# Self attention's first loads in order of use, with a semaphore for each group, in a two-layer decoder on one core

## The chip, the cores and the metric

The kernel runs on one core of one Trainium2 chip. The metric is the device time of one execution in microseconds; lower is better. All loads and stores of the part that matters here are issued by SyncE (SP) and are carried by the core's 16 DMA engines, which work through them while TensorE (PE), VectorE (DVE), ScalarE (ACT) and GpSimd (POOL) compute.

## The reference

The model is a decoder of two layers on x of 16 batches, 100 tokens and 256 features. Each sublayer adds its result to x and normalises. The parts run one after the other: self attention with four branches, cross attention, an expert adapter, a second attention in buckets, a latent attention and a routed feed-forward layer. The change touches only the first part (and the place where the last part's buffer is set to zero):

```python
q = (X @ Wq + bq).reshape(B, T, H_TOT, DH).transpose(0, 2, 1, 3)   # 64 heads of 16
v = (X @ Wv + bv).reshape(B, T, H_TOT, DH).transpose(0, 2, 1, 3)
k_base = (X @ Wk + bk).reshape(B, T, N_HEAD, DH).transpose(0, 2, 1, 3)
k = jnp.tile(k_base, (1, N_BR, 1, 1))
q = _rope(q); k = _rope(k)
scores = einsum('bhtd,bhsd->bhts', q, k) * ATTN_SCALE
w = jax.nn.softplus(scores / sqrt(clip(sum(k * k), 1e-06)))
w = jnp.where(causal, w, 0.0); w = w * jax.nn.sigmoid(SCALE * w)
sinks = jnp.tanh(sink_scalars) + 1e-06
alpha = 1.0 / (jnp.sum(w, axis=-1, keepdims=True) + sinks + 1e-06)
context = einsum('bhts,bhsd->bhtd', w * alpha, v) + sinks * alpha * v_nulls
y = context @ Wo + bo        # then the mean over the four branches
```

So k needs Wk, bk and the tables of the rotation, q needs Wq and bq, v needs Wv and bv, the scores need two masks, and the end of a batch needs Wo, bo, the sinks and v_nulls.

## The kernel before

Everything is float32 and is held in SBUF: `X` is [128, 16, 256], one batch per middle index. `build` (L2739 and on) first opens a block of its own ("io"). There DVE sets the tile `zero` to 0 (L2754), and SP issues the identity matrix `ident` (L2758), the whole of x (L2759, 1,600 KB), and then twenty stores of `zero` (L2762, 128 KB each) that clear `rows_in`, the DRAM buffer of the routed layer, which is used only at the end of the kernel. SP then waits for x (`s_in`), and the block ends with a barrier of all engines.

`self_attention` follows. SP issues 16 loads (L281), all on one semaphore `s_w`, then the operands of cross attention and of the router (L86). At their heads PE, DVE, ACT and POOL each wait for the full count of `s_w` (`16 * NW`): PE ahead of `x_turned(0)`, DVE after ten memsets and ahead of the constants, ACT ahead of the Tanh of the sinks (L676), POOL ahead of `staged(0)` (L683), which copies a batch of x for PE to transpose. DVE's constants are `odd` (L607), `sink` and `csk` (L608, L609) and `csvn` (L611, L613).

Then `four_in_flight` runs the same body on each engine, o = -3, -2, -1, 0 written out, ten in a hardware loop of two, five written out. In one body four batches are in work at different steps: F projects k and q of batch o + 3 and applies the rotation (POOL), S makes scores and masks of batch o + 2 and projects v, V multiplies the gated weights with v, O sums and normalises. The body o = -3 holds F alone, o = -2 holds F and S. On PE the body o = -3 is `k_projected` (L298), `q_projected` (L306), `k_turned` (L325), `q_turned` (L334), and the transposition of the next batch (L291); the body o = -2 begins with `scores` (L350). On DVE a body's order is masks, bias of k (L461), bias of q (L474), the sum of squares of k (L466, L468), masks (L500), v with its bias (L492), `kT_read` (L482), `xT_read` (L455), softplus (L507). On ACT: the copy of q (`qT_read`, L622), sigmoid (L629), logarithm (L633), gate (L637). The order on every engine is that of the program text; nothing is scheduled by a tool.

Of the kernel before, what the change touches and what calls it, by code (L numbers as in the profile page):

```python
# [14 lines left out]
P = 128  # L15
NB, T, D = 16, 100, 256
KD = D // P
NH = 16
# [179 lines left out]
def self_attention(nc, X, ident, d, later):  # L198
# [13 lines left out]
    with st:  # L212
# [35 lines left out]
        s_w, s_c = sem("weights_loaded"), sem("consts_ready")  # L248
# [17 lines left out]
        NW = 16  # L266

        with nc.Block() as block:
            @block.sync
            def _(sp):  # L270
                for dst, src in ((wk[:], rows(d["L0_attn_Wk"])), (bk[:], bcast(d["L0_attn_bk"], T)),
                                 (wq[:], rows(d["L0_attn_Wq"])), (bq[:], bcast(d["L0_attn_bq"], T)),
                                 (cos[:], d["c_cos"]), (sin[:], d["c_sin"]), (odd[:], d["c_odd"]),
                                 (wv[:], rows(d["t_L0_attn_Wv"])),
                                 (bv[0:HK, :], bcast(d["t_L0_attn_bv"][0, :], HK)),
                                 (bv[HK:P, :], bcast(d["t_L0_attn_bv"][1, :], HK)),
                                 (mask_a[:], d["c_mask_a"]), (mask_b[:], d["c_mask_b"]),
                                 (wo[:], rows(d["t_L0_attn_Wo"])), (bo[:], bcast(d["L0_attn_bo"], T)),
                                 (sink[:], bcast(d["t_L0_attn_sinks"], T)),
                                 (csvn[:], bcast(d["t_L0_attn_v_nulls"], T))):  # L280
                    sp.dma_start(dst, src).then_inc(s_w, 16)  # L281
                for w in later:
                    w.load(sp)

            @block.tensor
            def _(pe):
# [111 lines left out]
                def body(o, par):  # L398
                    N, F, S, V, O = parts(o)
                    f, s, v = o + 3, o + 2, o + 1  # L400
                    other = (par + 1) % 2
                    if S:
                        scores(s, par, 0)
# [40 lines left out]
                pe.wait_ge(s_w, 16 * NW)  # L444
# [4 lines left out]
            def _(dv):  # L449
# [99 lines left out]

                def body(o, par):  # L550
                    N, F, S, V, O = parts(o)
                    f, s, v = o + 3, o + 2, o + 1
                    other = (par + 1) % 2
                    if S:
                        masked(s, 0)
# [10 lines left out]
                    if F:  # L566
                        q_biased(f, 1)
                        k_summed(f)
                    if S:
                        masked(s, 2)  # L570
                        masked(s, 3)
# [24 lines left out]

                cs.start(0)
                for b in range(2):
                    nc.vector.memset(xT[b][:], 0.0)
                    nc.vector.memset(kTm[b][:], 0.0)  # L600
                    cs.after(nc.vector.memset(va[b][:], 0.0))
                    nc.vector.memset(va[b][:, :, :, DH:DH + 1], 1.0)
                nc.vector.memset(half[:], -0.5)
                cs.after(nc.vector.memset(tiny[:], 1e-37))
                dv.wait_ge(s_w, 16 * NW)
                dv.wait_ge(s_c, 1)
                cs.after(nc.vector.tensor_scalar(odd[:], odd[:], DH ** -0.5, None, ALU.mult))  # L607
                cs.after(nc.vector.tensor_scalar(sink[:], sink[:], 1e-6, None, ALU.add))  # L608
                cs.after(nc.vector.tensor_scalar(csk[:], sink[:], 1e-6, CS, ALU.add, ALU.mult))  # L609
                v3 = csvn[:, :].rearrange("p (h c) -> p h c", c=DH)  # L610
                cs.after(nc.vector.tensor_tensor(v3, v3, sink[:, :].unsqueeze(2).broadcast_to([T, NBR * NH, DH]),  # L611
                                                 ALU.mult))
                cs.after(nc.vector.tensor_scalar(csvn[:], csvn[:], CS, None, ALU.mult))  # L613
# [4 lines left out]
            def _(ac):  # L618
# [56 lines left out]
                ac.wait_ge(s_w, 16 * NW)  # L675
                nc.scalar.activation(sink[:], sink[:], ACT.Tanh).then_inc(s_c, 1)  # L676
# [3 lines left out]
            def _(po):  # L680
# [65 lines left out]
                def body(o, par):  # L746
                    N, F, S, V, O = parts(o)
                    f, s, v = o + 3, o + 2, o + 1
                    if F:
                        k_roped(f)  # L750
# [14 lines left out]
                po.wait_ge(s_w, 16 * NW)  # L765
                staged(0)
                four_in_flight(po, body)
# [1973 lines left out]
def build(nc, d, out):  # L2741
# [4 lines left out]
    with st:  # L2746
        X = st.sb("X", [P, NB, D])
        ident, zero = st.sb("ident", [P, P]), st.sb("zero", [P, D])
        s_in = st.sem("x_loaded")
        s_z, s_zero = st.sem("zero_ready"), st.sem("rows_zeroed")  # L2750
        with nc.Block() as block:
            @block.vector
            def _(dv):
                nc.vector.memset(zero[:], 0.0).then_inc(s_z, 1)  # L2754

# [82 lines left out]
```

## Time and profile before

| | us |
|---|---|
| median of 3 runs | 2407.62 (2407.28 to 2408.91) |
| the profiled execution | 2405.48 |
| its span, first to last instruction | 2403.8 |
| PE busy | 2046.5 (85% of the span) |
| the first projection starts at | 43.83 |

The profile has one execution. Its times count from the first instruction; 1.68 us of the profiled execution lie outside the span. Engines are named as above; SPq is SyncE's queue, whose instructions here only issue DMAs.

### The profile page before, as it was taken

The page shows a single profiled execution, that of the slowest core. Times are in us where ns is not written, and L with a number is a line of the kernel's source. Part 1 is how long each engine was busy: PE and PEld are TensorE (multiplying, and loading weights), DVE is VectorE, ACT ScalarE, POOL GpSimd, SP SyncE. Part 2 cuts the span into 40 slices and gives each one's busy share as a digit, 9 for nine tenths or more (in the row PEclk, how much of TensorE's full clock was granted, in tenths as well). Part 3 has the DMA queues.
Part 4 walks back from the last instruction along what each step waited for, and adds up shares of the span by engine and source line. Part 5 has one row for each costly group of instructions (what it writes and reads, how often), then busy time and mean ns, then how long its engine had stood idle before and what let it go on. Part 6 is the DMA issues. An engine that isn't in the chain of part 4 may idle for free. (4 is left out here: it accounts for less than half of the span.)

```text
span 2403.8 us, 48411 instructions
## 1 busy us (share of the span) xinstructions
PE 2046.5 (85%) x17362; PEld 1267.9 (53%) x17363; DVE 1345.4 (56%) x3265; ACT 1118.3 (47%) x2404; POOL 482.6 (20%) x583
## 2 busy tenths in 40 slices
PE   1788878869999997878879999999999999955991
PEld 0444445545666664645545555555555556543671
DVE  2577778744555555479954555555555555541223
ACT  0676677734555553346644444544444454420110
POOL 2566655510101000155520000000000000002002
PEclk9899999868999997889989999999999999967996
DMA  6000000003121000000000000000000000053102
GB/s 163 1 2 1 0 0 0 2 15 87 45 83 38 12 12 1 1 1 0 0 7 11 10 7 6 6 6 6 6 6 6 12 6 1 1 186 142 33 30 60
DMA packets 50463, 60.85 MB, mean 25 GB/s; under 512 B 9849, under 2 KB 44974, under 8 KB 49918
## 3 DMA queue, kind: packets, MB, share of 16 engines
q1 hardware_dynamic: 47366, 53.74, 7.2%
q0 software_dynamic: 3008, 5.91, 0.8%
q8 instruction: 57, 0.93, 0.2%
q14 instruction: 32, 0.26, 0.0%
HBM read 51.11 MB, written 8.52 MB: 25 GB/s over the span
## 5 line engine op out<-in xcount | busy, mean ns | idle before, releaser
L2011 PE MATMUL la_side<-la_wkv,la_inT 128*128 128x512 f32 (+1 forms) x512 | 243.8, 599 | 0.0
L2289 ACT COPY la_pT<-la_pPT 128x400 f32<-128x400 f32 x246 | 122.0, 496 | 257.4 <-PE la_pPT L2042 256.9
L1999 PE MATMUL la_side<-la_inT,la_wkv 128*128 128x461 f32 x512 | 225.6, 564 | 0.8 <-ACT la_inT L2264 0.8
L2179 DVE CUSTOM_DVE_ANT_0 la_pr<-la_pS,la_mb 100x461 f32<-100x461 f32 x256 | 148.1, 636 | 130.3 <-PE la_pS L2029 130.3
L2280 ACT ACTIVATE la_pr<-la_pr,la_nm 100x461 f32<-100x461 f32 x256 | 172.5, 681 | 0.0
L2353 POOL TENSOR_TENSOR la_xb<-io_X,la_bo 100x256 f32<-100x256 f32 x16 | 11.7, 730 | 784.2 <-DVE io_X L2168 784.2
L1020 DVE TENSOR_REDUCE ca_nm<-ca_pS 100x2 f32<-100x722 f32 x128 | 116.2, 908 | 85.9 <-PE ca_pS L907 84.1
L2042 PEld LDWEIGHTS la_pPT<-io_ident,la_pr 100*128 100x128 f32 x984 | 110.1, 141 | 102.5 <-issue 97.4
L2141 DVE COPY la_v<-la_side 128x512 f32<-128x512 f32 (+1 forms) x128 | 88.3, 690 | 130.9 <-PE la_side L2011 129.6
L1092 ACT ACTIVATE ca_pr<-ca_pS,ca_nm 100x361 f32<-100x361 f32 x256 | 130.0, 561 | 64.5 <-DVE ca_nm L1020 62.7
L2042 PE MATMUL la_pPT<-io_ident,la_pr 100*128 100x100 f32 x984 | 125.4, 249 | 1.4 <-issue 1.4
L1999 PEld LDWEIGHTS la_side<-la_inT,la_wkv 128*128 128x128 f32 x512 | 89.1, 193 | 67.2 <-issue 66.5
L2011 PEld LDWEIGHTS la_side<-la_wkv,la_inT 128*128 128x128 f32 (+1 forms) x512 | 82.7, 179 | 77.6 <-issue 77.6
L2029 PE MATMUL la_pS<-la_kT,la_qT 64*100 64x461 f32 x512 | 115.9, 571 | 0.0
L2268 ACT COPY la_kT<-la_side 128x461 f32<-128x461 f32 x128 | 68.8, 538 | 96.0 <-PE la_side L1999 96.0
L907 PE MATMUL ca_pS<-ca_kT,ca_qTm 32*100 32x361 f32 x512 | 110.2, 506 | 0.3
L2052 PEld LDWEIGHTS la_pav<-la_pT,la_v 128*64 128x64 f32 x2048 | 90.2, 137 | 37.9 <-issue 33.5
L2189 DVE TENSOR_SCALAR la_pr<-la_pr,la_zs 100x461 f32<-100x461 f32 x256 | 106.4, 458 | 4.5
L2052 PE MATMUL la_pav<-la_pT,la_v 128*64 128x100 f32 x2048 | 103.5, 253 | 3.1 <-ACT la_pT L2289 2.7
L1760 ACT ACTIVATE ba_pr<-ba_A,ba_mx 100x100 f32<-100x100 f32 x256 | 75.8, 367 | 53.1 <-DVE ba_mx L1702 53.1
L372 PEld LDWEIGHTS sa_pb<-sa_L,sa_va 64*32 64x32 f32 x4096 | 69.9, 110 | 53.8 <-issue 53.8
L916 PE MATMUL ca_pPT<-io_ident,ca_pr 100*128 100x100 f32 x768 | 88.5, 251 | 4.3 <-DVE ca_pT L1027 2.5
(360 smaller groups left out, 4225.7 us busy)
## 6 DMA issues: line engine op xcount, KB each, us to landing
rf_w<-in_L_ffn_W SPq DMA_DIRECT2D x16, 1024.0 KB, 13.2
ca_cn<-in_ctx SPq DMA_DIRECT2D x16, 256.0 KB
far_cn<-in_ctx SPq DMA_DIRECT2D x16, 256.0 KB, 2.7
rows_in<-io_zero SPq DMA_DIRECT2D x20, 128.0 KB, 4.7
rb_xr<-rows_in POOLq DMA_DIRECT2D x20, 128.0 KB, 2.3
rows_out<-rb_yr SPq DMA_DIRECT2D x20, 128.0 KB, 1.7
ea_wcT<-in_t_L_ffn_conv_W SPq DMA_DIRECT2D x1, 2048.0 KB
la_wkv<-in_L_xattn_Wkv SPq DMA_DIRECT2D x1, 2048.0 KB
```

The source lines that it names most:

```text
L907: last = nc.tensor.matmul(pS[0:T, 2 * (m % 2) + e, 0:SC], qTm[b][rows_, h // HG, h % 2, :], kT[b][rows_, h // HG, :], start=True, stop=True)
L1020: nc.vector.reduce_max(nm[m % 2][:], pS[0:T, 2 * (m % 2):2 * (m % 2) + 2, 0:SC], AX, negate=True)\
L1092: ins = nc.scalar.activation(pr[m % NP][:, e, 0:SC], pS[0:T, 2 * (m % 2) + e, 0:SC], ACT.Exp, bias=nm[m % 2][:, e:e + 1])
L1999: last = nc.tensor.matmul(pf[:, 0:SK], wkv[:, k, e * P:(e + 1) * P], inT[:, k, :], start=k == 0, stop=k == KD - 1)
L2011: last = nc.tensor.matmul(pf[0:keys[c], :], inT[:, k, c * P:c * P + keys[c]], wkv[:, k, o:o + 512], start=k == 0, stop=k == KD - 1)
L2029: last = nc.tensor.matmul(o[e], qT[b][half[e], m, :], kT[b][half[e], m, :], start=True, stop=True)
L2042: last = nc.tensor.transpose(dst[:, c * T:(c + 1) * T], pr[m % 4][:, e, c * P:(c + 1) * P], ident[0:T, 0:T])
L2052: last = nc.tensor.matmul(pav[DX * e:DX * (e + 1), m % 4, :], v[b][:, c, (2 * m + e) * DX:(2 * m + e + 1) * DX], pT[m % 2][:, e, c * T:(c ...
L2179: ins = nc.vector.tensor_tensor_reduce(out=pr[m % 4][:, e, 0:SK], in0=pS[0:T, 2 * (m % 2) + e, 0:SK], in1=mb[b][:, :], scale=-1.0, scalar= ...
L2189: ins = nc.vector.tensor_scalar(pr[m % 4][:, e, 0:SK], pr[m % 4][:, e, 0:SK], zs[m % 2][:, 2 + e:3 + e], None, ALU.mult)
L2280: ins = nc.scalar.activation(pr[m % 4][:, e, 0:SK], pr[m % 4][:, e, 0:SK], ACT.Exp, scale=-1.0, bias=nm[m % 2][:, e:e + 1], accum_out=zs[m ...
L2289: nc.scalar.copy(pT[m % 2][:, e, :], src[:, 0:NC * T]).then_inc(s_PT, 1)
```

## The change

Self attention takes over the io block's work, so that block and its barrier are gone. SP now issues, on seven semaphores: `ident` and batches 0 and 1 of x (`s_x0`); Wk, bk, cos, sin, odd (`s_lk`); Wq, bq (`s_lq`); Wv, bv, the masks (`s_lv`); the other 14 batches of x (`s_xl`); Wo, bo, sinks, v_nulls (`s_lo`); the operands of later stages as before; and the twenty stores of `zero` last. PE and POOL start on `s_x0`; the body o = -3 (`begin`) waits for k's and q's groups, the body o = -2 (`second`) for the rest. The memsets of `va` move into DVE's body o = -3, the constants from the sinks and v_nulls into its body o = -2, the Tanh to the head of ACT's body o = -2.

```diff
         with nc.Block() as block:
             @block.sync
             def _(sp):
+                xt = d["x"].rearrange("b t d -> t b d")
+                sp.dma_start(ident[:], d["c_ident"]).then_inc(s_x0, 16)
+                sp.dma_start(X[0:T, 0:2, :], xt[:, 0:2, :]).then_inc(s_x0, 16)
                 for dst, src in ((wk[:], rows(d["L0_attn_Wk"])), (bk[:], bcast(d["L0_attn_bk"], T)),
...
+                sp.dma_start(X[0:T, 2:NB, :], xt[:, 2:NB, :]).then_inc(s_xl, 16)
...
                 for w in later:
                     w.load(sp)
+                sp.wait_ge(s_z, 1)
+                for k in range(NBK):
+                    sp.dma_start(rows_in[k * P:(k + 1) * P, :], zero[:]).then_inc(s_zero, 16)
...
             def _(pe):
...
+                    if begin:
+                        pe.wait_ge(s_lk, 16 * 5)
+                        pe.wait_ge(s_lq, 16 * 2)
+                    if second:
+                        pe.wait_ge(s_lv, 16 * 5)
+                        pe.wait_ge(s_lo, 16 * 4)
...
-                pe.wait_ge(s_w, 16 * NW)
+                pe.wait_ge(s_x0, 32)
                 x_turned(0)
                 four_in_flight(pe, body)
...
             def _(dv):
...
+                def values_prepared():
+                    for b in range(2):
+                        cs.after(nc.vector.memset(va[b][:], 0.0))
+                        cs.after(nc.vector.memset(va[b][:, :, :, DH:DH + 1], 1.0))
+
+                def sinks_prepared():
+                    dv.wait_ge(s_lo, 16 * 4)
+                    dv.wait_ge(s_c, 1)
...
                     if F:
                         q_biased(f, 1)
                         k_summed(f)
+                    if begin:
+                        values_prepared()
+                    if second:
+                        sinks_prepared()
                     if S:
                         masked(s, 2)
...
             def _(ac):
...
+                    if isinstance(o, int) and o == FIRST + 1:
+                        ac.wait_ge(s_lo, 16 * 4)
+                        nc.scalar.activation(sink[:], sink[:], ACT.Tanh).then_inc(s_c, 1)
                     if V:
...
             def _(po):
...
+                    if second:
+                        po.wait_ge(s_xl, 16)
+                        po.wait_ge(s_lo, 16 * 4)
...
-                po.wait_ge(s_w, 16 * NW)
+                po.wait_ge(s_x0, 32)
                 staged(0)
+                po.wait_ge(s_lk, 16 * 5)
                 four_in_flight(po, body)
...
-        s_in = st.sem("x_loaded")
-        s_z, s_zero = st.sem("zero_ready"), st.sem("rows_zeroed")
-        with nc.Block() as block:
...
-                sp.dma_start(X[0:T, :, :], d["x"].rearrange("b t d -> t b d")).then_inc(s_in, 16)
-                sp.wait_ge(s_z, 1)
-                for k in range(NBK):
-                    sp.dma_start(rows_in[k * P:(k + 1) * P, :], zero[:]).then_inc(s_zero, 16)
-                sp.wait_ge(s_in, 32)
```

On SP, the queue from its start. Names are destination and source; `x19` is nineteen alike; before:

```order
L2758 DMA io_ident<-in_c_ident 128x128
L2759 DMA io_X<-in_x 100x16x256
L2762 DMA rows_in<-io_zero 128x256 [waits io_zero_ready]
L2762 DMA rows_in<-io_zero 128x256 x19
L2751 UNCONDITIONAL_BRANCH [waits io_x_loaded]
L269 UNCONDITIONAL_BRANCH [waits barrier_Pool_Activation_PE_DVE_SP_release]
L281 DMA sa_wk<-in_L_attn_Wk 128x2x256
L281 DMA sa_bk<-in_L_attn_bk 100x256
L281 DMA sa_wq<-in_L_attn_Wq 128x2x1024
L281 DMA sa_bq<-in_L_attn_bq 100x1024
```

and in the changed kernel:

```order
L274 DMA io_ident<-in_c_ident 128x128
L275 DMA io_X<-in_x 100x2x256
L278 DMA sa_wk<-in_L_attn_Wk 128x2x256
L278 DMA sa_bk<-in_L_attn_bk 100x256
L278 DMA sa_cos<-in_c_cos 100x8
L278 DMA sa_sin<-in_c_sin 100x8
L278 DMA sa_odd<-in_c_odd 128x2
L280 DMA sa_wq<-in_L_attn_Wq 128x2x1024
L280 DMA sa_bq<-in_L_attn_bq 100x1024
```

Wk was behind all of x, twenty stores, a wait and a barrier; it is now behind the identity and two batches of x.

On DVE, from the last setup to the first mask of the body o = -2, before:

```order
L607 TENSOR_SCALAR sa_odd<-sa_odd 128x2 [waits sa_consts_ready,sa_weights_loaded,sa_setup_chain]
L608 TENSOR_SCALAR sa_sink<-sa_sink 100x64 [waits sa_setup_chain]
L609 TENSOR_SCALAR sa_csk<-sa_sink 100x64 [waits sa_setup_chain]
L611 TENSOR_TENSOR sa_csvn<-sa_csvn,sa_sink 100x1024 [waits sa_setup_chain]
L613 TENSOR_SCALAR sa_csvn<-sa_csvn 100x1024 [waits sa_setup_chain]
L455 COPY sa_xT<-sa_pk 128x2x100 [waits sa_xT_in_psum,sa_setup_chain]
L461 TENSOR_TENSOR sa_kn<-sa_pk,sa_bk 100x256 [waits sa_k_in_psum]
L474 TENSOR_TENSOR sa_qn<-sa_pq,sa_bq 100x512 [waits sa_q_in_psum] x2
L466 TENSOR_REDUCE sa_kss<-sa_ksq 100x16 [waits sa_k_squares]
L468 TENSOR_SCALAR sa_kss<-sa_kss 100x16 [waits sa_k_sum_chain]
L482 TENSOR_TENSOR sa_kTm<-sa_pk,sa_odd 128x2x128 [waits sa_kT_in_psum]
```

and in the changed kernel, the same stretch:

```order
L648 TENSOR_SCALAR sa_odd<-sa_odd 128x2 [waits sa_k_operands_loaded,sa_setup_chain]
L474 COPY sa_xT<-sa_pk 128x2x100 [waits sa_xT_in_psum,sa_setup_chain]
L480 TENSOR_TENSOR sa_kn<-sa_pk,sa_bk 100x256 [waits sa_k_in_psum,sa_q_operands_loaded]
L493 TENSOR_TENSOR sa_qn<-sa_pq,sa_bq 100x512 [waits sa_q_in_psum] x2
L485 TENSOR_REDUCE sa_kss<-sa_ksq 100x16 [waits sa_k_squares]
L487 TENSOR_SCALAR sa_kss<-sa_kss 100x16 [waits sa_k_sum_chain]
L571 MEMSET sa_va 128x2048
L572 MEMSET sa_va 128x64 [waits sa_setup_chain]
L571 MEMSET sa_va 128x2048 [waits sa_setup_chain]
L572 MEMSET sa_va 128x64 [waits sa_setup_chain]
L501 TENSOR_TENSOR sa_kTm<-sa_pk,sa_odd 128x2x128 [waits sa_kT_in_psum,sa_setup_chain]
```

The four constants are gone from ahead of the first copy of x, and four memsets stand between the sum of squares of k and `kT_read`.

On DVE in the body o = -2, in the changed kernel; before, the mask L500 (here L519) followed the sum of squares directly:

```order
L485 TENSOR_REDUCE sa_kss<-sa_ksq 100x16 [waits sa_k_factors,sa_k_squares]
L487 TENSOR_SCALAR sa_kss<-sa_kss 100x16 [waits sa_k_sum_chain]
L577 TENSOR_SCALAR sa_sink<-sa_sink 100x64 [waits sa_consts_ready,sa_out_operands_loaded]
L578 TENSOR_SCALAR sa_csk<-sa_sink 100x64 [waits sa_setup_chain]
L580 TENSOR_TENSOR sa_csvn<-sa_csvn,sa_sink 100x1024 [waits sa_setup_chain]
L582 TENSOR_SCALAR sa_csvn<-sa_csvn 100x1024 [waits sa_setup_chain]
L519 TENSOR_TENSOR sa_sm<-sa_pS,sa_mask_a 128x800 [waits sa_scores_in_psum,sa_setup_chain]
```

The four constants now stand ahead of the masks of the third and fourth chunk.

## Rows read from the trace of the kernel before

**Rows 1.** Timeline, 0 to 31 us: start us, duration us, engine, line, operation.
```profile
1.02 0.27 DVE L2754 MEMSET io_zero<- 128x256 f32 x1 [1.02 <-PEq L2826]
1.35 0.39 SPq L2759 DMA_DIRECT2D io_X<-in_x  x1
1.80 14.73 SPq L2762 DMA_DIRECT2D rows_in<-io_zero  x20
16.98 0.40 SPq L281 DMA_DIRECT2D sa_wk<-in_L_attn_Wk  x1
...
20.27 0.27 DVE L599 MEMSET sa_xT<- 128x256 f32 x1
...
27.13 2.99 SPq L281 DMA_DIRECT2D sa_csvn<-in_t_L_attn_v_nulls  x1
```

**Rows 2.** Waits, 0 to 200 us: waiter, releaser, us, times, longest.
```profile
POOL sa_xs L683 <- DMA sa_csvn<-in_t_L_attn_v_nulls: 39.8, 1, 39.8
```

**Rows 3.** Timeline, 18 to 66 us: start, duration, engine, line, [idle before, releaser].
```profile
18.30 1.76 DVE L601 MEMSET sa_va<- 128x2048 f32 x1 [0.38 <-issue]
...
40.38 0.40 POOL L683 COPY sa_xs<-io_X 100x256 f32<-100x256 f32 x1 [39.79 <-DMA sa_csvn<-in_t_L_attn_v_nulls]
...
41.42 1.23 DVE L611 TENSOR_TENSOR sa_csvn<-sa_csvn,sa_sink 100x1024 f32<-100x1024 f32 x1
...
42.68 0.69 DVE L613 TENSOR_SCALAR sa_csvn<-sa_csvn 100x1024 f32<-100x1024 f32 x1
...
43.83 2.03 PE L298 MATMUL sa_pk<-sa_wk,sa_xT 128*100 128x256 f32 x4 [2.34 <-DVE sa_xT L455]
...
52.09 1.04 DVE L468 TENSOR_SCALAR sa_kss<-sa_kss 100x16 f32<-100x16 f32 x1
...
58.64 0.64 DVE L482 TENSOR_TENSOR sa_kTm<-sa_pk,sa_odd 128x256 f32<-128x256 f32 x2 [5.51 <-PE sa_pk L325]
...
65.79 1.34 PE L350 MATMUL sa_pS<-sa_qT,sa_kTm 32*128 32x144 f32 x16 [0.67 <-ACT sa_qT L622]
```

**Rows 4.** Windows: us, POOL busy (x), PEclk, DMA share, GB/s.
```profile
2.00:7.00 5.00, 0.00 (x0) 1.00 0.65 160
12.00:17.00 5.00, 0.00 (x0) 1.00 0.98 330
17.00:40.00 23.00, 0.00 (x0) 1.00 0.96 251
```

**Rows 5.** DMA issues: count, KB each, median us to landing.
```profile
rows_in<-io_zero SPq DMA_DIRECT2D x20, 128.0 KB, 4.7
io_X<-in_x SPq DMA_DIRECT2D x1, 1600.0 KB
```

**Rows 6.** Timeline of the body o = -2, 67 to 88 us.
```profile
67.98 0.68 ACT L629 ACTIVATE sa_L<-sa_sm 128x576 f32<-128x576 f32 x1 [1.03 <-DVE sa_sm L500]
...
74.93 1.30 POOL L729 TENSOR_TENSOR sa_qb<-sa_qn,sa_sin 100x512 f32<-100x512 f32 x1
...
82.39 1.26 ACT L633 ACTIVATE sa_L<-sa_L,sa_tiny 128x1152 f32<-128x1152 f32 x1
...
85.06 1.59 PE L334 MATMUL sa_pq<-io_ident,sa_qr 100*128 100x100 f32 x8 [4.80 <-POOL sa_qr L740]
...
86.69 0.83 ACT L622 COPY sa_qT<-sa_pq 128x800 f32<-128x800 f32 x1 [3.04 <-PE sa_pq L334]
```

**Rows 7.** Timeline, the same DVE line in two places, 100 to 107 us.
```profile
100.28 0.42 DVE L525 TENSOR_TENSOR sa_num<-sa_num,sa_alpha 100x256 f32<-100x256 f32 x1
...
105.41 1.30 POOL L736 TENSOR_TENSOR sa_qa<-sa_qn,sa_sin 100x512 f32<-100x512 f32 x1
...
105.70 1.29 DVE L525 TENSOR_TENSOR sa_num<-sa_num,sa_alpha 100x256 f32<-100x256 f32 x1
```

**Rows 8.** Windows, fill and loop: PE, PEld, DVE, ACT, POOL busy (x), PEclk, DMA share, GB/s.
```profile
40.40:66.00 25.60, 10.47 (x30) 5.45 (x34) 7.03 (x14) 1.37 (x3) 14.97 (x17) 0.80 0.05 11
...
154.00:198.00 44.00, 35.85 (x633) 22.18 (x632) 33.98 (x70) 30.65 (x33) 27.29 (x27) 1.00 0.01 2
```

More of the change, by code:

```diff
@@ L195, in four_in_flight, with self_attention @@
         body(o, o % 2)
-def self_attention(nc, X, ident, d, later):
+def self_attention(nc, X, ident, d, later, zero, rows_in, s_zero):
     CS = float(np.pi / np.sqrt(3.0))
@@ L246, in self_attention @@
         pb = ps("pb", [P, 512])
-        s_w, s_c = sem("weights_loaded"), sem("consts_ready")
+        s_x0, s_xl = sem("first_x_loaded"), sem("x_loaded")
+        s_lk, s_lq, s_lv, s_lo = (sem(f"{n}_operands_loaded") for n in ("k", "q", "v", "out"))
+        s_c, s_z = sem("consts_ready"), sem("zero_ready")
         s_xs, s_xTp, s_xT = sem("xs_staged"), sem("xT_in_psum"), sem("xT_ready")
@@ L401, in body @@
                     other = (par + 1) % 2
+                    begin, second = isinstance(o, int) and o == FIRST, isinstance(o, int) and o == FIRST + 1
+                    if begin:
[4 more added lines that the diff above has]
+                        pe.wait_ge(s_lo, 16 * 4)
                     if S:
@@ L548, in normed @@
                         .then_inc(s_x, 1)
+                def values_prepared():
[5 more added lines that the diff above has]
+                    dv.wait_ge(s_c, 1)
+                    cs.after(nc.vector.tensor_scalar(sink[:], sink[:], 1e-6, None, ALU.add))
+                    cs.after(nc.vector.tensor_scalar(csk[:], sink[:], 1e-6, CS, ALU.add, ALU.mult))
+                    v3 = csvn[:, :].rearrange("p (h c) -> p h c", c=DH)
+                    cs.after(nc.vector.tensor_tensor(v3, v3, sink[:, :].unsqueeze(2).broadcast_to([T, NBR * NH, DH]),
+                                                     ALU.mult))
+                    cs.after(nc.vector.tensor_scalar(csvn[:], csvn[:], CS, None, ALU.mult))
                 def body(o, par):
@@ L553, in body @@
                     other = (par + 1) % 2
+                    begin, second = isinstance(o, int) and o == FIRST, isinstance(o, int) and o == FIRST + 1
+                    if begin:
+                        dv.wait_ge(s_lq, 16 * 2)
+                    if second:
+                        dv.wait_ge(s_lv, 16 * 5)
                     if S:
@@ L595, in body @@
                         softplus(s, par, 2)
+                nc.vector.memset(zero[:], 0.0).then_inc(s_z, 1)
                 cs.start(0)
@@ L599, in _ @@
                     nc.vector.memset(xT[b][:], 0.0)
-                    nc.vector.memset(kTm[b][:], 0.0)
-                    cs.after(nc.vector.memset(va[b][:], 0.0))
-                    nc.vector.memset(va[b][:, :, :, DH:DH + 1], 1.0)
+                    cs.after(nc.vector.memset(kTm[b][:], 0.0))
                 nc.vector.memset(half[:], -0.5)
                 cs.after(nc.vector.memset(tiny[:], 1e-37))
-                dv.wait_ge(s_w, 16 * NW)
-                dv.wait_ge(s_c, 1)
+                dv.wait_ge(s_lk, 16 * 5)
                 cs.after(nc.vector.tensor_scalar(odd[:], odd[:], DH ** -0.5, None, ALU.mult))
[L608 to L613, printed above, removed]
                 xT_read(0, 0)
@@ L748, in body @@
                     f, s, v = o + 3, o + 2, o + 1
+                    second = isinstance(o, int) and o == FIRST + 1
+                    if second:
+                        po.wait_ge(s_xl, 16)
+                        po.wait_ge(s_lo, 16 * 4)
                     if F:
```

29 lines of the change are left out of this document (13 added, 16 removed).

## The prediction

> **What bounds the kernel at its start.** I read SyncE's queue first, then the waits, then the timeline of the first body. SyncE issues x at 1.35 us, then spends 14.73 us on the twenty stores of zeros (1.80 to 16.53), and the weights' first load leaves only at 16.98 [rows 1]. The waits say who suffers: POOL's first copy of x, and all behind it, waits 39.8 us for one load, v_nulls, the last of the sixteen that share one semaphore [rows 2]. In the timeline the last load has landed just ahead of 40.38, and PE's first projection starts at 43.83, 3.4 us later: between them stand the copy of x, its transposition, and DVE's constants, of which the last ends at 43.37 [rows 3]. So the kernel computes nothing of use in its first 43.83 us. What follows is a chain of stages with a barrier after each, none of which waits for something with a time of its own. Whatever the first projection gains, the end gains, less what the fill gives back.
>
> **Part 1: when k's and q's operands are there.** From the shapes (a tile's partitions times elements times 4 bytes; two of the sizes are in [rows 5]) the bytes ahead of `s_lq` are: identity 64 KB, two batches of x 200, Wk 256, bk 100, three small tables 7, Wq 1,024, bq 400: 2,051 KB or 2.10 MB. All six groups up to v_nulls are 5,580 KB, 5.71 MB. Before, 2,560 KB (2.62 MB) of zeros went with them, and everything had landed at 40.2.
>
> First what the removal of the zeros is worth. In the stretch 12 to 17 us, which is zeros almost alone, 330 GB/s moved [rows 4]: 2.62 MB are 7.9 us. So the last group should land at 40.2 - 7.9 = 32.3 us; SyncE's first load leaves at about 1 us as before and moves its first bytes at about 2.0. That is 5.71 MB in 30.3 us, 188 GB/s. The first 2.10 MB at that rate take 11.2 us and land at 13.2. At the 251 GB/s of the stretch 17 to 40 us [rows 4] they take 8.4 us and land at 10.4. The stretch 2 to 7 us, x almost alone, moved only 160 GB/s with a DMA share of 0.65 [rows 4], so I stay near the slow end: 12.5, with 10.4 and 13.2 as near bounds. A far bound: the three stretches of [rows 4] moved 0.80, 1.65 and 5.77 MB, and the one between them (7 to 12 us), at 160 to 330 GB/s, 0.8 to 1.65: by 40 us 9.0 to 9.9 MB had moved, against 8.34 MB issued up to v_nulls. So some 1.1 MB of later loads were ahead of it, and a group doesn't land strictly first; 1.1 MB more at 188 GB/s make 19.
>
> The DMA share of 0.65 with x alone [rows 4] is what 10 busy engines of 16 give. The Trainium skill (DMA: Bandwidth & Descriptors, "Why a DMA increments its semaphore by 16 and not by 1") says that a transfer with 100 partitions is split over 10 engines and one with 128 over 16, and the trace agrees. By that rule the ten engines carry 155 KB each up to `s_lq` and 447 KB each up to `s_lo`; 155/447 of 30.3 us would be 10.5 us, a landing at 12.5. By bytes alone it is 13.2; the page would leave the sum where it is.
>
> What else stood ahead of the projection is covered: the identity and two batches of x (264 KB) land at some 4 us, so POOL's copy, PE's transposition and DVE's memsets (all but `va`'s) are done long before 12.5, and the small k group lands before the large q group. The first projection starts at 12.6 instead of 43.83: **31.2 us gained**.
>
> **Part 2: the second body's wait.** PE waits for `s_lv` and `s_lo` at the head of the body o = -2, ahead of `scores`. Behind it in its queue are the scores, the k and q projections and everything that feeds DVE and POOL. ACT waits for `s_lo` after its first copy of q. These stood at 65.79 [rows 3], 21.96 us after the first projection, so they come up at 12.6 + 22.0 = 34.6. The last group lands at 32.3 by part 1: 2.3 us early, cost nothing. This cover is thin. The gain at that point is 65.8 less the later of (the landing of `s_lo`) and (the landing of `s_lq` + 22.1). If q's group comes at 10.4 the second wait binds, and the gain is 33.5 and not more; if `s_lo` comes at 36 it is 29.8. POOL's wait for `s_xl` and `s_lo` has more room: its next work is the first multiplication after the bias of k, well after the scores.
>
> **Part 3: DVE's memsets of `va` in the body o = -3.** Two of 1.76 us [rows 3] and two small ones (64 elements each, under the 0.27 us of a memset of 256 [rows 1]), with their chain waits some 4.2 us. They start when the sum of squares ends, at 53.13, and DVE was idle from there until 58.64, 5.51 us [rows 3]. 5.5 against 4.2 to 4.9: cost 0. If each stood behind a POOL operation of 1.3 us once, they would end up to 1 us late: bound 1.0.
>
> **Part 4: the constants in the body o = -2.** Before, the two long ones ran from 41.42 to 43.37 [rows 3], with the two small ones ahead of them 2.4 us in all, after POOL's copy. Now they run from about 75.0 (times of before) beside POOL's 1.30 us multiplication at 74.93 [rows 6]. The pair L525/L736 shows what that does: the same DVE operation takes 0.42 us alone and 1.29 beside POOL's, ending when POOL's ends [rows 7]; L468, a sum's clip over 16 elements, takes as much as 1.04 beside POOL in the first body [rows 3]. So the masks behind the constants move by 2.4 to 3.7 us. Who waits: the scores of the third group on PE, then sigmoid and logarithm on ACT. ACT's logarithm ended at 83.65 and ACT then idled 3.04 us until the copy of q at 86.69 [rows 6]. The shift is at most 3.5 there (0.2 is taken up by DVE's own idle time): 0 to 0.5 us too late. The other way round, DVE's two long operations (1.23 and 0.69 [rows 3]) can hold up POOL, and PE does wait for POOL's chain (4.80 us ahead of L334) [rows 6]: up to 1.9 us. I take 0.5 for both together, near the low end, since POOL's next operation after 76.2 reads only 16 elements a partition.
>
> The Trainium skill (SBUF — State Buffer, the part on the shared port pair) says that a DVE operation with two SBUF inputs, or a `tensor_scalar` in the fast mode, and a GpSimd operation that reads SBUF exclude each other, while a memset doesn't contend. The 1.29 of [rows 7] agrees; that a memset is free of it no row shows. By the page part 3 costs nothing and part 4 is as above.
>
> **Part 5: what moves without a price.** The Tanh (0.26 us) stands before the first sigmoid, for which ACT waited 1.03 us [rows 6]; no table load is added. The zeros leave at some 35 to 50 us, behind the operands of later stages; nobody needs them before the last stage. The DMA queue is then full while bodies -3 to -1 run; before, it was nearly idle there (share 0.05 [rows 8]). DVE's memset of 256 elements took 0.27 us both at 1.02, before any byte had moved, and at 20.27 in the full stretch [rows 1, 4], so I put nothing on it. Below zero nothing is to be had: no operation left out was on the path apart from those of part 1.
>
> **The sum.** 31.2 - 0.5 = 30.7 us. The profiled execution, 2405.48 with a span of 2403.8, becomes 2374.8 with a span of 2373.1. The median of the runs is 2.14 us above the profiled execution, 2407.62; it becomes **2376.9 us**.
>
> **The rivals.**
> 1. *The second wait takes the place of the first.* The last group lands later than 34.6, since the first 25 us now hold only loads and no fast zeros. For it: the margin is 2.3 us out of 32. Against it: the same loads with the zeros between them took 40.2. Landing at 36 to 38 gives a gain of 29.8 to 27.8, less 0.5: 2378.3 to 2380.3. It decides from 34.6 on.
> 2. *The fill gives back more.* Parts 3 and 4 at their upper bounds (1.0 + 0.5 + 1.9 = 3.4), or PE's clock comes up later in the first body (there it was granted 0.80 on average [rows 8], between its two levels of 1.2 and 2.4 GHz; eight q matmuls at most 1.7 us slower). Gain 31.2 - 3.4 = 27.8: 2379.8.
> 3. *The groups don't land apart.* If the queue works on all issued loads at once, q's group lands almost with the last, at 32.3, and only the zeros and the constants are saved: 43.83 - 32.4 = 11.4 us gained: 2396.2. For it: the 1.1 MB of part 1 that overtook. Against: that is an eighth of the traffic then, not all of it.
> 4. *Slower.* The loop of self attention loses its clock. It runs at 1.00 with PE busy 35.85 of 44 us [rows 8]. PE rests longer ahead of its first work in one piece no more, but the fill now begins with a transposition at 4 us and a pause until 12.6; if the grant in the loop fell to the lower level, the 35.85 us would become 71.7, 27.7 us more than the stretch of 44. It would turn the gain into a loss after some 49 us of such running: 2,407 and above, 2420 for 70 us. Against it: before, the clock came up after a far longer pause.
>
> **How the numbers follow.** The forecast 0.70, second wait 0.12, fill 0.10, groups together 0.05, slower 0.03. The forecast's own bounds: gain 33.5 (q at 10.4) less 0 is 2374.1; q at 13.2 with 1 us of fill is 2378.1; another 1 us on both sides for clock and run. The range of 8 in 10 takes in rivals 1 and 2: 2373 to 2381. A measurement of this kernel can tell about 0.2% (4.8 us) from no change; only rival 4 reaches that bound from the other side: faster 0.96, same 0.01, slower 0.03.
>
> **What will show it.** Right: the first projection at 12.6 (10.4 to 13.3) with PE released by a load of the q group; SyncE's zeros last; the scores L350's counterpart at 34.6 released by ACT's copy of q and not by a DMA; ACT's idle before the second copy of q down from 3.0 to near 0; the memsets done before `kT_read`; everything from 110 us on as before, 30.7 earlier. Wrong: a DMA as releaser at the scores (rival 1), POOL operations of over 1.3 us beside DVE's constants or a late `kT_read` (rival 2), the projection after 20 us (rival 3), a PEclk below 1.00 in the loop (rival 4).

## The result, and the profile after

The changed kernel takes **2384.57 us** (median of 4 executions, 2382.62 to 2391.57) against 2408.01 of the kernel before; the ratio is 0.9899, with a 95% interval of 0.9879 to 0.9919. That is faster, by 23.4 us in the medians where 30.7 were forecast, and outside the range of 2373 to 2381. The profiled execution took 2382.62 us with a span of 2381.0, 22.8 us less than before.

The start of the changed kernel, in the order of time: start, duration, engine, line, operation, [idle before, releaser]. These rows answer to [rows 1], [rows 3] and [rows 6].

```profile
0.88 0.42 SPq L274 DMA_DIRECT2D io_ident<-in_c_ident  x1
...
4.68 0.40 POOL L719 COPY sa_xs<-io_X 100x256 f32<-100x256 f32 x1 [4.09 <-DMA io_X<-in_x]
...
8.20 8.01 SPq L290 DMA_DIRECT2D sa_wo<-in_t_L_attn_Wo  x1
11.64 2.00 PE L310 MATMUL sa_pk<-sa_wk,sa_xT 128*100 128x256 f32 x4 [5.86 <-DMA sa_bq<-in_L_attn_bq]
...
21.44 1.76 DVE L571 MEMSET sa_va<- 128x2048 f32 x1 [0.37 <-issue]
...
23.93 1.76 DVE L571 MEMSET sa_va<- 128x2048 f32 x1 [0.49 <-DVE sa_va L572]
...
26.65 0.64 DVE L501 TENSOR_TENSOR sa_kTm<-sa_pk,sa_odd 128x256 f32<-128x256 f32 x2 [0.73 <-PE sa_pk L337]
...
31.79 9.70 SPq L295 DMA_DIRECT2D rows_in<-io_zero  x20
...
33.73 1.34 PE L362 MATMUL sa_pS<-sa_qT,sa_kTm 32*128 32x144 f32 x16 [0.67 <-ACT sa_qT L657]
```

The first projection is at 11.64 us and is released by the last load of q's group: 32.2 us earlier than in [rows 3]. The scores of the second body are at 33.73, released by ACT's copy of q and by no DMA, 32.1 us earlier. Up to here the prediction holds.

To see where the gain went, take an instruction of DVE that both traces have (PE's first projection in the first line) and subtract its starts; call the difference the gain at that place. The places are named by their time before:

| place (time before) | gain, us |
|---|---|
| PE's first projection (43.8) | 32.2 |
| end of the fill (125) | 31.4 |
| late loop of self attention (310 to 415) | 32.9 |
| first bias of q in cross attention (about 540) | 32.8 |
| cross attention, its fill done (612) | 28.4 |
| end of cross attention (914) | 28.4 |
| latent attention (1,500 to 2,069) | 27.1 |
| behind latent attention (2,130) | 22.2 |
| routed layer (2,200 to 2,318) | 23.6 |
| end of the span | 22.8 |

It is a staircase, flat for hundreds of microseconds, with single steps, most of them down and a few up. The two large ones, -4.4 us around 555 and -4.9 us around 2,100, are in stages that the change doesn't touch. The first 45 us of cross attention, from its first load on, are this row in the kernel before (stretch, length, PE busy and instructions, PEclk, DMA share, GB/s):

```profile
528.70:573.70 45.00, 37.23 (x160) 0.68 0.32 91
```

and this in the changed kernel:

```profile
495.80:540.80 45.00, 37.74 (x138) 0.55 0.32 91
```

The DMA columns are the same, and the clock that TensorE was granted is not: 0.68 of full against 0.55, that is less of the stretch at 2.4 GHz and more at 1.2. The end of latent attention before:

```profile
2069.00:2130.00 61.00, 47.42 (x422) 0.95 0.00 1
```

and in the changed kernel, where the same 422 matmuls take 66 us:

```profile
2042.00:2108.00 66.00, 53.08 (x422) 0.86 0.00 1
```

The question for the chip is whether this is a fixed cost of the change (theory B), or whether the clock is just at its lower level over another piece of work whenever the work arrives at another time (theory A).

### The profile page after: what moved, and what is told of

Read it like the earlier page. It is cut to its first block and busy times, and to the rows that moved or that the text cites. A ratio compares the mean times of both kernels' runs of the same rounds, so it can differ in the third digit from the quotient of the medians.

```text
span 2381.0 us, 48409 instructions
## 1 busy us (share of the span) xinstructions
PE 2056.3 (86%) x17362; PEld 1272.5 (53%) x17363; DVE 1346.7 (57%) x3265; ACT 1119.3 (47%) x2404; POOL 482.9 (20%) x583
## 5 line engine op out<-in xcount | busy, mean ns | idle before, releaser
L2093 PEld LDWEIGHTS la_pav<-la_pT,la_v 128*64 128x64 f32 x2048 | 92.0, 139 | 37.3 <-issue 33.5
```

The costliest lines, as they stand in the source:

```text
L2093: last = nc.tensor.matmul(pav[DX * e:DX * (e + 1), m % 4, :], v[b][:, c, (2 * m + e) * DX:(2 * m + e + 1) * DX], pT[m % 2][:, e, c * T:(c ...
```

## The experiments

In all of them the kernel before ran on the same chip beside the variants. In four series of measurements, each on one chip, it had 63 executions, from 2403.55 to 2420.58 us, with medians of 2408.45, 2412.41, 2409.72 and 2414.30.

### The changed kernel again

> The changed kernel once more, to be compared with the other runs of this call. Theory A (clock): the loads' new order gains about 32 us up to the first scores and keeps it to the end of self attention; what is lost behind it is lost where TensorE's granted clock stands at its lower level over another piece of the work, so its executions scatter: times from 2380 to 2392, and stages that keep or lose single pieces of 1.5 to 5 us against the first profile. Theory B (a fixed cost of the change behind self attention): the same 28.4 us of gain left in cross attention and the same 22 to 23 at the end as in the first profile, 2383 to 2385.

Measured: 2385.88 us (2385.48 to 2387.89, 4 executions), ratio 0.9906 (0.9888 to 0.9923). Its profiled execution has a gain of 32.6 at the scores, 29.5 at the end of the fill, 27.2 at the start of cross attention and 22.9 behind its fill, and 17.6 at the end. So theory B's fixed 28.4 in cross attention is out, and theory A's range holds; but the step in cross attention's fill is -4.3 us again, at the same share of clock (0.55).

### Only the zeros moved

```diff
@@ the kernel before, io block and self attention's loads
-                for k in range(NBK):
-                    sp.dma_start(rows_in[k * P:(k + 1) * P, :], zero[:]).then_inc(s_zero, 16)
                 sp.wait_ge(s_in, 32)
...
                 for w in later:
                     w.load(sp)
+                for k in range(NBK):
+                    sp.dma_start(rows_in[k * P:(k + 1) * P, :], zero[:]).then_inc(s_zero, 16)
```

> The kernel before with one part of the change: the twenty stores of zeros are issued behind all loads of self attention's block; the io block, its barrier, the one semaphore and DVE's constants stay. x lands at about 10 us, the sixteen loads are issued from there, and by 251 GB/s of the full stretch their 4.0 MB and the waits behind them put the first projection at 30 to 35 us instead of 43.8: 9 to 14 us gained there. Theory A: the end is that gain give or take 5 us, 2392 to 2402. Theory B, if the zeros' new place is the fixed cost: 5 to 10 us less gain at the end than at the first projection, and all of it lost at the same places as in the changed kernel.

Measured: 2409.84 us (2403.44 to 2412.18), ratio 0.9999 (0.9987 to 1.0012). SyncE and PE:

```profile
1.35 0.39 SPq L2761 DMA_DIRECT2D io_X<-in_x  x1
16.19 0.41 SPq L281 DMA_DIRECT2D sa_wk<-in_L_attn_Wk  x1
```

```profile
41.88 2.03 PE L300 MATMUL sa_pk<-sa_wk,sa_xT 128*100 128x256 f32 x4 [2.34 <-DVE sa_xT L457]
```

Without the zeros the weights still leave only at 16.19 (16.98 before): x by itself lasts that long, and SyncE now waits 14.0 us for it, until just before it leaves the block:

```profile
SPq L2763 <- DMA io_X<-in_x: 14.0, 1, 14.0
```

In the kernel before, SyncE had no such wait, since issuing the stores kept it until 16.53 [rows 1]. The windows say why x lasts (PEclk, DMA share, GB/s are the last three columns):

```profile
2.00:7.00 5.00, 0.00 (x0) 1.00 0.61 133
7.00:12.00 5.00, 0.00 (x0) 1.00 0.70 153
```

With x alone the DMA share is 0.61 to 0.70 and 133 to 153 GB/s move. The zeros had filled what x left unused. Moving them alone is worth 1.95 us at the first projection, not the 9 to 14 of my expectation, and nothing that can be measured in the median. Theory A's range for the end, 2392 to 2402, took that gain for granted and was missed.

### The groups undone

```diff
                 pe.wait_ge(s_x0, 32)
+                pe.wait_ge(s_lk, 16 * 5)
+                pe.wait_ge(s_lq, 16 * 2)
+                pe.wait_ge(s_lv, 16 * 5)
+                pe.wait_ge(s_xl, 16)
+                pe.wait_ge(s_lo, 16 * 4)
                 x_turned(0)
```

The same five waits stand on POOL ahead of its first copy.

> The changed kernel with the groups undone: PE and POOL wait for all six groups ahead of the first transposition; order of loads, zeros last, constants in the fill all as in the changed kernel. This measures when the last group lands, which nothing in the changed kernel waits for. By the prediction it lands at 32.3 us, so the first projection is at 33.5 to 34.5 and the gain there some 10 us; if groups were overtaken by later loads as in rival 3, the same landing would have shown in the changed kernel, which it did not. Theory A: 2393 to 2403 in the end. Theory B: 10 us less gain at the end than at the first projection.

Measured: 2404.72 us (2399.86 to 2408.6), ratio 0.9983 (0.9971 to 0.9996). POOL's first copy and PE's first projection:

```profile
30.80 0.39 POOL L724 COPY sa_xs<-io_X 100x256 f32<-100x256 f32 x1 [30.21 <-DMA sa_csvn<-in_t_L_attn_v_nulls]
```

```profile
32.53 2.00 PE L310 MATMUL sa_pk<-sa_wk,sa_xT 128*100 128x256 f32 x4 [0.62 <-DVE sa_xT L479]
```

The last group lands just before 30.8, where I had put 32.3. Of the 32.2 us at the first projection, 20.9 come from the groups (32.53 to 11.64) and 11.3 from all the rest (43.83 to 32.53). In this rest, 9.6 us are the earlier landing of the last load (POOL's first copy at 30.80 and not at 40.38), which the order, the io block that is gone and the zeros give together; the other 1.7 are DVE's constants, which no longer stand between that copy and the projection (3.45 us then, 1.73 now). At the end of its profiled execution nothing is left of the 11.3 (its span is 3.1 us longer than that of before), and that execution was the slowest of its ten. In the medians of the series 3.7 us are left. Theory A's range for the end, 2393 to 2403, was missed; that some 10 us of the gain would be lost was theory B's forecast.

### The zeros put back in front, in the changed kernel

```diff
                 sp.dma_start(X[0:T, 0:2, :], xt[:, 0:2, :]).then_inc(s_x0, 16)
+                sp.wait_ge(s_z, 1)
+                for k in range(NBK):
+                    sp.dma_start(rows_in[k * P:(k + 1) * P, :], zero[:]).then_inc(s_zero, 16)
...
-                sp.wait_ge(s_z, 1)
-                for k in range(NBK):
-                    sp.dma_start(rows_in[k * P:(k + 1) * P, :], zero[:]).then_inc(s_zero, 16)
```

> The changed kernel with one part undone: the twenty stores of zeros stand right behind the first two batches of x, ahead of the weights. By the prediction's part 1 (zeros are worth their bytes at 330 GB/s, 7.9 us) q's group lands 7.9 us later, and the first projection is at 19.5 us. By what the run with only the zeros moved showed (1.95 us at the first projection), the stores fit into time that the queue had anyway, and the first projection is at 13.5 to 14. The end follows, give or take the clock: 2388 to 2396 by the first, 2381 to 2392 by the second.

Measured: 2389.49 us (2388.67 to 2396.91), ratio 0.9904 (0.9877 to 0.9931).

```profile
1.79 9.83 SPq L278 DMA_DIRECT2D rows_in<-io_zero  x20
11.66 0.45 SPq L281 DMA_DIRECT2D sa_wk<-in_L_attn_Wk  x1
```

```profile
21.36 2.00 PE L310 MATMUL sa_pk<-sa_wk,sa_xT 128*100 128x256 f32 x4 [15.66 <-DMA sa_bq<-in_L_attn_bq]
```

The first projection is 9.7 us later than in the changed kernel, nearly the 9.83 us for which SyncE issues the stores, and later than both forecasts, 19.5 and 13.5 to 14. The median lies in the first range, 2388 to 2396. The same twenty stores cost 1.95 us behind all of x and 9.7 us behind two batches of it: in the first order they hid beside a transfer that lasts as long, in the second they stand ahead of what is waited for.

### The start delayed, in both kernels

```diff
+                cs.after(nc.vector.memset(L[0][:, 0:2048], 0.0))    # once, twice or four times
                 xT_read(0, 0)
                 four_in_flight(dv, body)
```

In the changed kernel this stands behind a wait for q's group. The memset writes a tile that is written again before it is read.

> The kernel before with one added memset of 2,048 elements (1.76 us and its chain wait) on DVE ahead of the first copy of x: everything behind it starts some 2.1 us later, and nothing of the change is in it. Theory A (the clock falls on other pieces of work when the work arrives at other times): the end moves by 2.1 us with 2 to 6 us up or down, and the profile shows single steps at the ends of self attention, at the start of cross attention and at the end of latent attention, as the changed kernel shows them. Theory B (the change itself costs some 10 us behind self attention): 2.1 us later, 2410 to 2411, no steps.

> The kernel before with two such memsets, some 4.3 us later. Theory A: between 2407 and 2418, with steps at other places than in the run with one. Theory B: 2412 to 2413.

> The changed kernel with one added memset of 2,048 elements (1.76 us) on DVE between the landing of q's group and the first copy of x, so that all work behind it moves by about 2.3 us (memset, its chain wait, and the copy of x which stood ahead of the landing); nothing else differs. Theory A: the end doesn't move by 2.3 us but by 2.3 with 2 to 6 us up or down, since the lower clock falls on other pieces of work. Theory B: 2.3 us later within 1 us, at every stage.

> The changed kernel with two added memsets between the landing of q's group and the first copy of x, some 4.4 us later. Theory A: 2384 to 2398, and not in proportion to the delay: it may end ahead of the run with one memset. Theory B: 4.4 us behind the changed kernel, 2389 to 2391.

> The changed kernel with four added memsets, some 8.5 us later at the first projection. Theory A: 2386 to 2401, steps at other places. Theory B: 2393 to 2396.

| run | executions, us | ratio | gain of the profiled one: scores, into cross attention, behind its fill, latent, end |
|---|---|---|---|
| before, 1 memset | 2412.03 (2404.24 to 2421.43) | 1.0003 (0.9984 to 1.0022) | -1.4, -1.2, -1.2, -1.0, -2.2 |
| before, 2 memsets | 2411.27 (2406.7 to 2418.81) | 1.0001 (0.9985 to 1.0018) | -3.4, **-7.8, -9.4**, -9.2, -10.1 |
| changed, 1 | 2393.99 (2382.15 to 2398.88) | 0.9929 (0.9905 to 0.9953) | 26.6, 18.5, **22.2**, 18.1, 12.1 |
| changed, 2 | 2387.94 (2386.05 to 2389.4) | 0.9893 (0.9876 to 0.9909) | 27.8, 19.9, 18.2, 17.3, 16.1 |
| changed, 4 | 2397.54 (2392.93 to 2401.8) | 0.9933 (0.9915 to 0.9951) | 23.8, 18.8, 14.4, 12.8, 6.3 |

Two things stand out. A delay of 3.4 us in the kernel before costs nothing in the median, and in the changed kernel two memsets are ahead of one, though the intervals of these two just touch: the medians do not follow the start. (The range of theory A was wide enough to take in all five runs. One memset in the kernel before decides nothing: its profile has a single step, -2.0 us at the end of latent attention.) And the kernel before, with nothing of the change in it, shows the same kind of step: in its profiled execution with two memsets it lost 4.9 us from the late loop (gain -2.9) to the start of cross attention and 1.6 more in its fill. Its row for the first 45 us of cross attention:

```profile
536.30:581.30 45.00, 37.28 (x151) 0.62 0.32 91
```

How long cross attention's fill takes goes by the granted share, whichever kernel it is in (change of the gain from 540 to 612, against the profile of before):

| PEclk over 45 us | runs | change of gain |
|---|---|---|
| 0.55 | changed in all three profiles, changed + 4 memsets, zeros in front | -4.4, -4.3, -4.4, -4.4, -4.3 |
| 0.62 | groups undone, changed + 2 memsets, before + 2 | -1.4, -1.7, -1.6 |
| 0.68 | before, zeros moved, before + 1 | 0, 0.1, 0.0 |
| 0.77 | changed + 1 | +3.7 |

In the run with one memset in the changed kernel the delay was not the one that was meant: q's group itself landed at 15.1, some 3.4 us later than in the two profiles of the changed kernel so far, so that its first projection is at 17.42 and not near 14.

### The clock held up by added matmuls

If the clock is the cause, work that keeps it up must bring the gain back, in both kernels. Matmuls whose result nothing reads were put where PE waits: in the last two bodies of self attention, and ahead of each of the eight steps that fill cross attention.

```diff
+                def filler(n):
+                    pe.wait_ge(s_sm, NB * NCH)
+                    for _ in range(n):
+                        nc.tensor.matmul(pS[:, 0, :], ident[:, :], wv[:, 0, 0:512], start=True, stop=True)
...
+                    tail = isinstance(o, int) and o >= NB - 2
+                    if tail:
+                        filler(1)    # at seven places of the body
...
                 for name, n in side.prologue():
+                    for _ in range(6 if n == 0 else 2):
+                        nc.tensor.matmul(pS[:, 0, 0:D], ident[:, :], wkT[:, 0, :], start=True, stop=True)
                     step(name, n, 0, 0)
```

> The changed kernel with matmuls added whose result nothing reads (identity by a weight, 128x512 in the last two bodies of self attention, 128x256 ahead of the eight steps of cross attention's fill), placed where TensorE waits. Theory A (behind the loads the time is set by where TensorE's clock stands at its lower level): the stretch at 0.5 from the end of self attention to about 45 us into cross attention gets shorter or goes, cross attention keeps what self attention gained, 30 us and more against the profile of before, and the end is 8 to 18 us ahead of the changed kernel: 2368 to 2378. Theory B (a fixed cost of the change there, not the clock): the added work helps nothing, 2385 or later, up to 8 us later for the added matmuls.

> The kernel before with the same added matmuls. Theory A: it gains too, 5 to 15 us, 2396 to 2405, and it stands 28 to 33 us behind the same addition to the changed kernel, which is what the loads' order is worth when the clock doesn't interfere. Theory B: no gain, and the difference to the changed kernel with the addition stays 22 to 25 us.

Measured: the changed kernel with them 2371.65 us (2371.27 to 2372.33, ratio 0.9845, 0.9822 to 0.9869), the kernel before with them 2404.52 (2400.9 to 2406.32, ratio 0.9977, 0.9961 to 0.9992). Between the two lie **32.9 us**; at their first projections (43.99 and 11.72) it was 32.3. The first 45 us of cross attention in the changed kernel with them:

```profile
501.50:546.50 45.00, 42.49 (x295) 1.00 0.37 102
```

and in the kernel before with them:

```profile
530.90:575.90 45.00, 42.47 (x258) 0.92 0.32 91
```

The first stays at 2.4 GHz through the fill, although PE has more to do. A single projection step of the fill in the changed kernel:

```profile
504.23 2.77 PE L911 MATMUL ca_side<-ca_cT,ca_WkT 128*128 128x361 f32 x4 [0.54 <-DVE ca_qb L1019]
```

and with the added matmuls:

```profile
509.44 1.38 PE L931 MATMUL ca_side<-ca_cT,ca_WkT 128*128 128x361 f32 x4
```

The added work is not free. Cross attention's first load is at 501.50, 5.7 us later than in the changed kernel, and the gain, 27.2 there, is 36.3 behind the fill.

The four executions of this kernel lie within 1.1 us of each other; the kernel before scatters over 17. It is the fastest of all kernels here: in the same series it is 8.2 us ahead of the changed kernel (2379.84) and 38.1 ahead of the one before (2409.72).

### A third measurement of the changed kernel

> The changed kernel a third time, for its spread and for one more profile of where the lower clock falls. Theory A: executions from 2380 to 2396, median 2384 to 2388, against a kernel before whose own executions lie between 2404 and 2419. Theory B: all within 2 us of 2384.

Measured: 2379.84 us (2378.69 to 2385.37, 5 executions), ratio 0.9883 (0.9861 to 0.9905). Its profile has 0.55 in cross attention's fill again (-4.4 us) and loses only 1.4 us at the end of latent attention, where the other two lost 4.9. Theory B's 2384 within 2 us is out, but theory A's median of 2384 to 2388 was missed as well, by 4 us on the fast side. Medians of the changed kernel in three series: 2384.57, 2385.88, 2379.84.

## Why the prediction was right, and where it failed

**Part 1, the landing of q's group: right in size, wrong in one of its reasons.** 12.5 was forecast for the landing, 12.6 for the projection, with near bounds of 10.4 and 13.2; the projection was at 11.64, 11.77 and 11.57 in three profiles. But "what the removal of the zeros is worth" was not 7.9 us: it was 1.95 taken alone and 9.7 in the new order. The step treated the queue as a pipe that is always full; [rows 4] had the answer, 0.65 of the DMA engines with x alone. What it left without a price is the time that SyncE spent in the io block, which kept the first weights until 16.98; in the changed kernel they leave at 1.78. The last group landed 9.6 us earlier than before, and the forecast had 7.9 for another reason. That the sum came out so near is in part luck. (A slip beside it: with q's group at 10.4 the prediction's own formula gives 32.5 for the scores, behind the last group's 32.3, so that the second wait wouldn't bind and the bound is 33.3 us of gain, not 33.5.)

**Part 2, the second wait: right.** Nothing waited for it. The last group lands before 30.8 in the run with the groups undone, the scores came up at 33.73: 2.9 us of cover, 2.3 forecast. In the other two profiles of the changed kernel they came up at 33.10 and 32.28, released by ACT there too. Rival 1 didn't occur, nor did rival 3.

**Part 3, the memsets of `va`: right, 0.** They ran from 21.44 to 25.92, each 1.76 us as in [rows 3], although POOL worked beside them, and `kT_read` still waited 0.73 us for PE. What the prediction took from the Trainium skill (SBUF — State Buffer), that a memset doesn't contend with GpSimd, held, now with a row.

**Part 4, the constants: right.** These are DVE's rows in the second body:

```profile
42.93 0.18 DVE L577 TENSOR_SCALAR sa_sink<-sa_sink 100x64 f32<-100x64 f32 x1
42.95 1.33 POOL L765 TENSOR_TENSOR sa_qb<-sa_qn,sa_sin 100x512 f32<-100x512 f32 x1
43.15 1.18 DVE L578 TENSOR_SCALAR sa_csk<-sa_sink 100x64 f32<-100x64 f32 x1
44.24 2.92 POOL L741 TENSOR_TENSOR sa_kf<-sa_kss,sa_half 100x16 f32<-100x16 f32 x1
44.36 1.23 DVE L580 TENSOR_TENSOR sa_csvn<-sa_csvn,sa_sink 100x1024 f32<-100x1024 f32 x1
45.62 0.69 DVE L582 TENSOR_SCALAR sa_csvn<-sa_csvn 100x1024 f32<-100x1024 f32 x1
46.35 1.89 DVE L519 TENSOR_TENSOR sa_sm<-sa_pS,sa_mask_a 128x800 f32<-128x800 f32 x2
```

The second constant took 1.18 us instead of 0.20 and ended when POOL's operation did (the pair in [rows 7], which the prediction read so, ends 0.3 us apart); the two long ones ran at their own length (1.23 and 0.69 us, as in [rows 3]) beside POOL's 16-element power. Here the trace doesn't bear out the other half of that passage of the Trainium skill, that a DVE operation with two SBUF inputs and a GpSimd operation that reads SBUF exclude each other: POOL's began first, at 44.24, and DVE's two-input operation didn't wait for its end at 47.16. The masks moved by 3.4 us (gain 32.0 ahead of them, 28.6 behind), 2.4 to 3.7 forecast. On ACT the cover of 3.04 us in [rows 6] is gone, as foreseen:

```profile
54.18 1.26 ACT L668 ACTIVATE sa_L<-sa_L,sa_tiny 128x1152 f32<-128x1152 f32 x1
55.35 0.81 ACT L657 COPY sa_qT<-sa_pq 128x800 f32<-128x800 f32 x1
```

The gain at this copy is 31.3 (86.69 to 55.35), so the price was 0.6 where 0.5 stood in the sum.

**The step that failed** is the sentence of the first part, "Whatever the first projection gains, the end gains, less what the fill gives back", together with its size in the numbers, "another 1 us on both sides for clock and run". The chain of stages has no time of its own, but the clock has. Where the sum of known terms has 30.7, the gain at the door of cross attention was 32.8 in the first profile and 32.1 in the third. Behind it the changed kernel lost 4.3 to 4.4 us in cross attention's fill, some 1.3 on the way to latent attention and 1.4 to 4.9 at its end, in stages that aren't touched. In the second profile only 27.2 were left at that door: 3.2 had gone in self attention's own fill and 2.3 at its end. Rival 2 had the clock, but only in the first body and at 1.7 us; rival 4 had it in the loop, where all traces stand near 1.00, and overlooked the stages' starts and ends, where PE pauses. [rows 8] showed the loop and the first bodies; a window over 500 to 600 us of the same trace would have shown how much was at stake:

```profile
500.00:600.00 100.00, 79.79 (x721) 0.76 0.22 61
```

**A second, smaller part** is the base. The sum was made against one execution of 2405.48 us, and the range against runs within 1.6 us of each other. With 63 executions the kernel before lies between 2403.55 and 2420.58: its profile was one of the better ones. The three comparisons, each side by side on one chip, give 23 to 30 us of gain in the medians; the sum of the known terms was 30.7.

**What the granted share makes of all executions.** Every execution comes with its mean granted share, and not only the profiled ones. Over the 63 executions of the kernel before, it runs from 0.932 to 0.942, and the time falls with it along a straight line, 1.3 us for each 0.001; around this line they scatter by 1.7 us (standard deviation), without it by 4.4. So the unchanged kernel's own spread goes with the clock. Compared with this line at the same share, the 13 executions of the changed kernel are 30.9 us ahead on average, where the sum had 30.7; the run with the groups undone is 9.4 ahead (11.3 at its first projection), the one with the zeros back in front 21.7 (22.5), and the kernel before with one and two memsets is 1.6 and 3.9 behind (1.7 and 4.1). The other four kernels without added matmuls lie within 3 us of their gain at the first projection. The delay that cost nothing in the median was thus paid, in executions whose share was higher (0.938 on average) than that of the kernel before in the same series (0.936). These are estimates from the times and shares of the executions, not an experiment; the share counts the idle start as full clock, which makes about 1 us of difference between the kernels.

What is shown: the same kind of loss occurs in the kernel before when its start moves by 3.4 us (0.62 instead of 0.68, and the piece at the end of self attention); the length of cross attention's fill goes with the granted share over all kernels; and with the clock held up there, the two kernels differ by 32.9 us. What stays open: why the changed kernel had 0.55 in three profiles of three, while the kernel before and its relatives had 0.68 and 0.62. The runs with delays show that it isn't tied to the change, since the changed kernel with one memset had 0.77, but five profiles with 0.55, all of kernels with the new order, are more than I can call chance. And the fill of self attention lost 0.6 us in the first profile of the changed kernel and 3.2 in the second. The granted share differs there as well, 0.98 in the first and 0.90 in the second:

```profile
60.00:100.00 40.00, 32.82 (x528) 0.98 0.01 2
59.00:99.00 40.00, 33.13 (x456) 0.90 0.01 2
```

No run tests this place apart.

## What to carry to other kernels

Loads in the order of use with a semaphore for each group are worth nearly the whole wait (32 us of 44 here), and most of it comes from the groups; moving a bulk store alone is worth what the transfer beside it leaves, here 2 us. What a start gains is kept in time by every stage, but not by TensorE's clock: read the granted share at the start and end of each stage, for both kernels, before promising the gain at the end, and compare executions at the same share. Where PE waits in the fill of a stage, matmuls that nobody reads can pay for themselves: here 8 us against the median of the changed kernel in the same series, with a spread of 1 us instead of several, and 5 us in the kernel before.

## What was not expected of the hardware

- x, 1,600 KB in 100 partitions, used 0.61 to 0.70 of the DMA engines in 2 to 12 us, where it was alone, and its block lasted to 16.19 us; with 2.62 MB of stores beside it the block lasted to 16.98. The ten engines of sixteen that the Trainium skill gives such a transfer (DMA: Bandwidth & Descriptors, "Why a DMA increments its semaphore by 16 and not by 1") would be 0.63; the trace agrees.
- SyncE was held at one issue for 8.01 us behind the second part of x (L290 in the changed kernel), with q's and v's groups already issued.
- The same loads in the same order landed at different times: q's group at about 11.6 us in three profiles of the changed kernel and at 15.1 in the run with one memset behind it.
- TensorE was busy 37.7 of 45 us and was granted 0.55 of its clock in the changed kernel, and 37.1 of 45 with 0.77 in the run with one memset; with 42.5 of 45 busy it was granted 1.00 in one kernel and 0.92 in the other. The busy share of a stretch doesn't tell the granted one.
- DVE's two-input operation over 1,024 elements took 1.23 us beside POOL's 16-element power, as long as without it.
